# Four chained cross-attention layers on one core: in the fourth layer, values are computed three steps ahead instead of two, the second keys' bias moves, and two activation tables are loaded by one-column activations

## The reference, cut to what matters

```python
qh = (q_in @ wq + bq).reshape(b, q_len, H, K)
kh = (kv_in @ wk + bk).reshape(b, t, H, K)
vh = (kv_in @ wv + bv).reshape(b, t, H, K)
kh = jnp.concatenate([kh, jnp.broadcast_to(bias_k, (b, 1, H, K))], axis=1)
vh = jnp.concatenate([vh, jnp.broadcast_to(bias_v, (b, 1, H, K))], axis=1)
logits = jnp.einsum('bqhk,bthk->bhqt', qh, kh) / scale
weights = jax.nn.softmax(logits, axis=-1)
ctx = jnp.einsum('bhqt,bthk->bqhk', weights, vh).reshape(b, q_len, H * K)
return ctx @ wo + bo
```

## Time and profile before

| what | value |
|---|---|
| median of three runs | 1078.21 us (1077.7 to 1078.83) |
| the profiled execution: its time | 1079.97 us |
| the profiled execution: span from first to last instruction | 1078.1 us |
| PE busy | 1009.2 us (94%) |
| DVE, ACT, POOL busy | 653.7 (61%), 512.3 (48%), 402.0 (37%) us |
| mean granted TensorE clock | 0.987 |

### The profile page before, as it was taken

One profiled execution on the slowest core, in us unless ns is written; L12 is line 12 of the kernel. 1 busy time (PEld: TensorE's weight loads), 2 busy tenths in 40 slices (PEclk: granted clock), 3 DMA queues, 4 the chain that ended last, 5 costly groups with the idle time before them and its releaser, 6 DMA issues.

```text
span 1078.1 us, 18116 instructions
## 1 busy us (share of the span) xinstructions
PE 1009.2 (94%) x7252; PEld 790.8 (73%) x7252; DVE 653.7 (61%) x1119; ACT 512.3 (48%) x1026; POOL 402.0 (37%) x424
## 2 busy tenths in 40 slices
PE   6999999997898898999999999999999999989997
PEld 3666566555566798987777777778777777769997
DVE  4757999885588678545453446765444544565552
ACT  2556898875485644434333233323323332345542
POOL 2444689898676334101221123332112212353110
PEclk9999999999799999999999999999999999999999
DMA  9102000000000510020000023110000000200000
GB/s 333 46 1 79 1 1 1 2 1 2 1 1 1 198 58 1 1 79 1 1 2 1 1 79 135 61 40 1 1 1 1 1 1 1 78 1 11 20 21 30
DMA packets 17463, 34.90 MB, mean 32 GB/s; under 512 B 3554, under 2 KB 8420, under 8 KB 16740
## 3 DMA queue, kind: packets, MB, share of 16 engines
q1 hardware_dynamic: 17380, 33.75, 9.1%
HBM read 31.65 MB, written 2.10 MB: 31 GB/s over the span
## 4 chain that ended last, share of the span: by engine, by line
PE 76%; POOL 7%; DVE 6%; ACT 6%; issue 4%; DMA 0%; SPq 0%; POOLq 0%; DVEq 0%; ACTq 0%
PE work L938 11%; PE work L815 10%; PE scores L874 10%; PE work L891 5%; PE work L927 4%; PE work L674 3%; PE work L676 3%; PE work L675 3%; PE scores L674 3%; PE scores L676 3%; PE scores L675 3%; PE work L539 3%; PE work L601 2%; POOL pair L1960 2%; PE work L909 2%
## 5 line engine op out<-in xcount | busy, mean ns | idle before, releaser
L938 PE MATMUL work<-pair,probsT 128*128 128x256 f32 x512 | 118.8, 385 | 11.1 <-ACT pair L1833 8.9
L1919 POOL TENSOR_SCALAR stat<-stat 128x2 f32<-128x2 f32 (+1 forms) x49 | 11.2, 228 | 302.9 <-DVE stat L1060 301.9
L938 PEld LDWEIGHTS work<-pair,probsT 128*128 128x128 f32 x512 | 94.6, 190 | 34.9 <-issue 20.4
L815 PE MATMUL work<-ctxT,w 128*128 128x128 f32 x992 | 116.1, 275 | 1.8 <-ACT pair L1833 1.1
L815 PEld LDWEIGHTS work<-ctxT,w 128*128 128x128 f32 x992 | 114.5, 192 | 3.0 <-ACT pair L1833 1.3
L874 PE MATMUL scores<-pair,act_bufs 128*128 128x512 f32 x256 | 115.2, 592 | 0.0
L1824 ACT ACTIVATE pair<-work 128x512 f32<-128x512 f32 x64 | 38.3, 598 | 160.2 <-PE work L891 160.2
L1814 ACT ACTIVATE kvT<-work,cols 128x128 f32<-128x128 f32 x120 | 34.3, 369 | 142.1 <-PE work L815 142.1
L2073 POOL TENSOR_TENSOR probs<-probs,smax 128x1024 f32<-128x1024 f32 x22 | 42.0, 1909 | 150.8 <-DVE smax L1449 150.8
L1429 DVE TENSOR_REDUCE smax<-scores 128x16 f32<-128x1024 f32 x32 | 39.2, 1225 | 79.6 <-PE scores L874 79.6
L874 PEld LDWEIGHTS scores<-pair,act_bufs 128*128 128x128 f32 x256 | 46.3, 190 | 46.0 <-issue 45.9
(11 more groups left out here) (190 smaller groups left out, 2555.1 us busy)
## 6 DMA issues: line engine op xcount, KB each, us to landing
w<-in_l_wk SPq DMA_DIRECT2D x8, 512.0 KB, 6.6
w<-in_l_wq SPq DMA_DIRECT2D x8, 512.0 KB, 7.1
w<-in_l_wo SPq DMA_DIRECT2D x8, 512.0 KB, 7.5
w<-in_l_wv SPq DMA_DIRECT2D x8, 512.0 KB, 5.1
x<-in_x SPq DMA_DIRECT2D x1, 2048.0 KB, 12.7
out<-x SPq DMA_DIRECT2D x8, 256.0 KB, 2.1
pair<-in_xT SPq DMA_DIRECT2D x1, 1536.0 KB, 6.9
pair<-in_l_fc SPq DMA_DIRECT2D x1, 1024.0 KB, 5.0
```

What stands on the lines that cost most here:

```text
L815: last = mm(bank[:, h * P:(h + 1) * P], w[:, c, (4 * g + h) * K3:(4 * g + h + 1) * K3], ctxT[:, c, p * P:(p + 1) * P], start=(c == 0), sto ...
L938: last = mm(step_banks(j + 1)[0][:, 0:D], probsT_bufs[j % 2][:, q, :], pv[n % 2][:, bb, q, :], start=(q == 0), stop=(q == GH // 2 - 1))
```

## The change

Four edits. **Values:** `value_of` and `values_before` become `j + 3`, so value group `i` is made in step `i - 3` (first in step -3, last in step 28); DVE's bias and ACT's copies read the banks of step `i - 3`. **Loads:** the loop that loads the second attention's weights has five rounds instead of six, with the value and output weights one round earlier. **Second keys:** ACT's `key_bias(0)` and `key_bias(1)` both stand ahead of the steps, and so ahead of the copies of the first keys' products. **Tables:** a new tile `scratch` of one column is written twice by ACT: with the tanh GELU ahead of the MLP of l2, and with Exp behind `key_bias(1)`.

```diff
+        scratch = sb("scratch", [P, 1])
         probs_late = sb("probs_late", [P, GS + H3])
         def value_of(j):
-            return j + 2 if 0 <= j + 2 < 8 * PAIRS else None
+            return j + 3 if 0 <= j + 3 < 8 * PAIRS else None
         def values_before(j):
-            return min(max(j + 2, 0), 8 * PAIRS)
+            return min(max(j + 3, 0), 8 * PAIRS)
-            for g in range(6):
+            for g in range(5):
                 if g < 4:
                     e.wait_ge(pe_pk, 2 * (last + g) + 2)
                     load_w3(2, g, "kq")
-                if g >= 2:
-                    e.wait_ge(pe_pv, 2 * (last + g - 2) + 2)
-                    load_w3(2, g - 2, "vo")
+                if g >= 1:
+                    e.wait_ge(pe_pv, 2 * (last + g - 1) + 2)
+                    load_w3(2, g - 1, "vo")
...
-                v.tensor_tensor(kvT[2][:, :, :], step_banks(i - 2)[1][:, :].rearrange("p (h s) -> p h s", h=4),
+                v.tensor_tensor(kvT[2][:, :, :], step_banks(i - 3)[1][:, :].rearrange("p (h s) -> p h s", h=4),
...
+            act(scratch[:, :], tanh_gate[:, :], ACT.Gelu_apprx_tanh)
             for b in range(B):
                 for f in range(3):
                     mlp_hidden(b, f)
...
-                        step_banks(i - 2)[2 + q][:, :].rearrange("p (b d) -> p b d", b=2), ACT.Copy).then_inc(a_pv, 1)
+                        step_banks(i - 3)[2 + q][:, :].rearrange("p (b d) -> p b d", b=2), ACT.Copy).then_inc(a_pv, 1)
...
+            key_bias(0)
+            key_bias(1)
+            act(scratch[:, :], tanh_gate[:, :], ACT.Exp)
             for j in STEPS:
                 key, value = key_of(j), value_of(j)
                 if key is not None:
-                    key_bias(key)
+                    if key >= 2:
+                        key_bias(key)
                     key_products(key)
```

## The result

| | before | changed |
|---|---|---|
| median of the runs taken together | 1078.12 us (1077.7 to 1078.83, 4 runs) | 1071.55 us (1069.28 to 1073.29, 4 runs) |
| ratio | | 0.9937, 95% interval 0.9913 to 0.9961 |
| the same, repeated with more runs | 1078.98 us (1077.95 to 1080.08, 17 runs) | 1070.82 us (1069.31 to 1072.73, 6 runs) |
| ratio | | 0.9926, 95% interval 0.9914 to 0.9938 |
| profiled execution: span | 1078.1 us | 1067.5 us |

The change makes the kernel 6.6 us faster in the first comparison and 8.2 in the second; 9.3 were forecast, and both medians lie in the range. In the two profiled executions it is 10.6 us, and 3.0 of these stand in the three first layers, where the change was to make nothing shorter, as the next table shows.

The account below looks back on a forecast made before the run. TensorE bounds steps 0 to 27 (busy 428.39 of 436.00 us, waits 7.6 us). Terms -1.28 - 1.5 + 4.45 + 1.5 - 1.05 - 6.55 - 4.85 = -9.3 us gave 1068.9 us, range 1066.0 to 1072.8.

Parts of the forecast that it names:

- GELU table (part 1): MLP of l2: table load moves into ACT's idle time, -1.28 us; half-clock stretch behind TensorE's wait gone, -1.5 us.
- Start (part 2): Steps -4 to -1: moved value work and a wait for value weights, +4.45 us; one half-clock stretch, +1.5 us.
- Exp (part 3): Step 0: with the Exp table load gone, value copies end before TensorE wants the bank, -1.05 us.
- Pairs (part 4): Steps 1, 5, ... 25: output products no longer wait for ACT's value copies, -7 x 0.94 = -6.55 us.
- the rival of another wait in its place: Pairs: probability copies or the product bank end just as late, 6.55 us stay, 1075.5 us; chance 0.06.
- Tail (part 5): Steps 28 to 31: step 29 gains 5.25 us, POOL's late deviation takes some back, -4.85 us (bounds -3.3, -5.25).
- that rival: Start: the four value-weight loads land together, costing 4.7 us more, 1073.6 us; chance 0.08.
- a drain with the tables: GELU table: a switch costs more than its load row, gaining up to 1.4 us more, 1067.5 us; chance 0.04.
- moved tiles that lose speed: First three layers and steps: the new column moves later tiles, DVE slows, 1082 us at 2%; chance 0.03.
- POOL bounding the tail: Tail: steps 30 and 31 wait for what step 29 saves, only 1 of 4.85 us left, 1072.8 us; chance 0.07.

Follow-up runs that it names:

- experiment 6: Changed kernel with POOL's eight last weight remainders moved behind tile 29's and tile 31's probabilities, batch 1's reciprocal deviation ahead of them: 1069.09 us, ratio 0.9910.
- Experiment 4: Changed kernel with the second key products ahead of the first value projection on TensorE in step -3: 1067.78 us, ratio 0.9908.
- experiment 1: Kernel before with values three ahead and the five-round load loop, without the three activations moved or added: 1073.15 us, ratio 0.9955.
- experiment 8: Kernel before (values two ahead) with moved key bias and one-column activations, the output's waits taken in parts: 1061.89 us, ratio 0.9843.
- experiment 5: Changed kernel with POOL's reciprocal deviation for batch 1's last norm ahead of its last four weight remainders: 1068.47 us, ratio 0.9914.
- experiment 3: Kernel before with the one-column GELU alone: 1077.13 us, ratio 0.9983.
- bias and tables: Kernel before with the second keys' bias moved and the two one-column activations, values two ahead: 1071.29 us, ratio 0.9937; run again, 1073.92 us, ratio 0.9951.

## Why the prediction was right, point by point

The range held both medians, and the sign, the start, the Exp load and the pairs came out as forecast; the GELU part was right in its wait alone, and the tail was mis-sized. The forecast of -9.3 us was 1 to 3 us too good. Some luck is in the hit: of the first four runs, two (1073.01 and 1073.29) lie above the range's 1072.8, and what parts them from the other two is not the change but the clock (0.986 against 0.990). Against the stages:

- **GELU table (part 1): right in the wait, wrong in the clock.** The wait fell by 1.24 us where 1.28 were forecast; the rest of the stage's 2.30, 1.06 us, is the clock, for which 1.5 were credited by the length of the wait ("nearest to the 2.35 that did not lower it"). That step failed as a rule: the half clock did go from behind this wait, but in five of eleven traces it came back at 435 us, behind a wait of 1.78 us, and behind the start's 2.87 us it came or stayed away. In those traces the credit is -0.8 us for the stage, not -2.8. The length of a wait alone does not tell, and the trace of the kernel before already had a row that says so: its wait of 2.36 us in the last MLP was followed by half clock. What else decides it these runs don't show.
- **Start (part 2): right.** +5.64 for +5.95. The weights held TensorE for 2.90 us in place of 3.37, and the half clock behind it was there. Of the 5.64 us, the idle time is 0.35 (2.90 for 2.55), the half clock 1.66 by experiment 6, and the moved work the remaining 3.6, where 0.8, 1.5 and 3.65 were forecast. Experiment 4 wins back a part of the first two. The loads stand under the new activations (354.31 and 457.11 us), where ACT would be idle, and cost nothing.
- **Exp (part 3): -0.88 for -1.05.** A wait of 0.17 us stays.
- **Pairs (part 4): -6.84 for -6.55.** All seven waits went, and each took about 0.04 us more with it than its idle time: from the value products of step 1 to the next projection it is 6.41 us before (511.43 to 517.84) and 5.43 now (510.91 to 516.34), 0.98 less. What the 0.04 are, no row shows; with them the steps gained a little more than the 7.6 us that the prediction called all there is. Experiments 1 and 8 remove them in two ways and reach the same 426.28 us beside the tables; so the profile's releaser was the right one, and the rival of another wait in its place falls.
- **Tail (part 5): mis-sized, -3.29 for -4.85.** This is the failed step. The forecast had POOL's late deviation right (2.22 us of wait on DVE for 2.1) but took POOL's remainders as a queue only. They also stopped DVE's small operations: with step 29 shorter, tile 29's clamp and its negated maximum fell together with the first four remainders, and took 0.79 and 1.28 us in place of about 0.2. That made the 0.67 us wait in step 30 that was not forecast, and the one in step 31 became 0.85 instead of 0.4; step 29 itself took 8.77 us, as forecast, but steps 30 and 31 became 0.88 and 1.06 us longer than before. That the lower bound of the term, -3.3, is what came is luck: it was put there for the whole 2.1 us of DVE's wait (5.25 - 2.1 would be 3.15), not for this. Experiments 5 and 6 part the two causes. (the earlier trace rows show two waits of 0.7 us for the transposed probabilities, in steps 30 and 31; the third that the prediction reads from them lies behind 970 us.)
- **The rivals.** The loads landed as the forecast had them, so that rival falls; a drain with the tables falls by experiment 3 and by the Exp switch of step 0; moved tiles that lose speed fall, for up to the first GELU DVE's 401 operations took 272.49 us before and 272.41 with the new column, and the ACT operation of the earlier trace rows takes 1058 ns on both tiles. POOL bounding the tail is true for about 1.5 of 4.85 us.
- **Not in the forecast:** the half clock in the first layers and in the last MLP, worth up to 2.5 and 1.5 us of a single run. Changed or not, a run can have it or lack it. It is why medians of a few runs lie some 2 us off the sum of their stages, as the first one of bias and tables did.

## What to carry to other kernels

Where an accumulating product waits for many inputs, let each product wait for its own input before moving the producer to an earlier step: the wait in parts gave the whole gain of the steps here, while the earlier step paid more than 5 us at the start, with moved work and with weights that had not landed. When a stretch gets shorter, look at what runs on the neighbouring engines in the same microseconds, not only at their queues: DVE's 0.17 us operations became 1.28 us beside POOL. Compare stages cut at the same instructions, since a median of a few runs of this kernel moves by some 3 us with the clock alone.

## What the runs showed of the hardware that was not expected

A switch of activation tables cost its load of 1.28 us and no more, where ACT had been idle before it (1.24 us of wait came back) and where it had just finished a copy (1.31 us from the copy to the exponentials). TensorE's granted clock fell to 0.50 behind a wait of 1.78 us at 436 us in one variant and stayed at 1.00 behind a wait of 1.72 us at the same place in the kernel before; behind the same 2.9 us wait for the value weights it fell in the changed kernel and did not in experiment 6; behind the same 2.36 us in the last MLP it fell in seven of thirteen traces. At 436 us, at the start and in the last MLP such a stretch cost 1.5 to 1.7 us. A tensor-scalar operation on 128 x 16 numbers, 0.17 us alone, took 0.57 to 1.28 us beside POOL's tensor-tensor instructions of 1.24 us and ended with one of them, and DVE's tensor-tensor operation on scores in PSUM kept its 1.22 us in the same stretch.
